# AdaLN block on one NeuronCore: latent scores in two row halves, first norm on ScalarE, new instruction lists and PSUM banks, expert weights mixed by quarters of the hidden layer

## The reference

```python
mod = (silu(c) @ wmod).reshape(32, 6, 1, 128)      # sa, ca, ga, sb, cb, gb
h = layernorm(x) * (1 + ca) + sa
x = x + ga * attn(h)
h = layernorm(x) * (1 + cb) + sb
x = x + gb * ffn(h)
# attn: 16 heads of 8, causal window of 32 over blocks of 32 keys, softmax;
#   8 latent heads: GQ = h@wgq, GK and GV = h@wgk and h@wgv pooled by 4 rows to 64 latents,
#   causal softmax over the latents, @ r_out_w; both gated by a sigmoid of Q, summed, @ w_out
# ffn: g = mean over rows of (relu(h@gate_w1.T + b) @ gate_w2.T + b2)      # 8 experts
#   mW1 = W1 + sum_e g[e] * TW1[e]   (512 x 128, one for each image)
#   mW2 = W2 + sum_e g[e] * TW2[e]   (128 x 512, one for each image)
#   out = gelu(h @ mW1.T + mb1) @ mW2.T + mb2
```

## Time and profile before

| | |
|---|---|
| median of 3 runs | 707.37 us (706.54 to 707.58) |
| the profiled execution: its own time | 706.55 us |
| the profiled execution: first to last instruction | 704.7 us, TensorE's clock granted at 0.983 of full on the mean |
| busy: PE, DVE, ACT, POOL | 662.0, 542.8, 382.1, 217.1 us |

### The profile page before, as it was taken

The page is one execution under the profiler, slowest core; times in us unless marked ns, Lnnn a source line. Parts: engine busy times, 40 slices in busy tenths (PEclk is TensorE's granted clock), DMA queues, the critical chain, the costliest instruction groups (busy, mean ns, idle before and its releaser), DMA issues.

```text
span 704.7 us, 24615 instructions
## 1 busy us (share of the span) xinstructions
PE 662.0 (94%) x9075; PEld 503.2 (71%) x9075; DVE 542.8 (77%) x1242; ACT 382.1 (54%) x907; POOL 217.1 (31%) x351
## 2 busy tenths in 40 slices
PE   4698999999999999999999999999869999999998
PEld 2365676667766667776667666677559899998996
DVE  5777898999998999999999989998757255472552
ACT  2264666567766577765677665677522423324232
POOL 3344444344533345443345443454320000000000
PEclk9799999999999999999999999999979999999999
DMA  4656410110011110101100101100500110000001
GB/s 108 170 79 87 57 31 22 30 30 22 22 30 24 34 24 22 30 22 28 32 22 22 30 22 30 30 15 16 74 3 2 30 32 7 30 22 30 30 8 52
DMA packets 65797, 24.84 MB, mean 35 GB/s; under 512 B 38440, under 2 KB 64360, under 8 KB 65648
## 3 DMA queue, kind: packets, MB, share of 16 engines
q1 hardware_dynamic: 64320, 18.25, 10.7%
q0 software_dynamic: 1456, 6.31, 5.8%
HBM read 16.13 MB, written 8.40 MB: 35 GB/s over the span
## 4 chain that ended last, share of the span: by engine, by line
PE 78%; DVE 16%; issue 3%; ACT 1%; DMA 0%; POOL 0%; DVEq 0%; SPq 0%; POOLq 0%
PE SB L822 8%; PE WB L810 8%; PE SB L889 7%; DVE rden L639 7%; PE WB L975 7%; PE WB L921 5%; PE WB L940 5%; PE WB L797 4%; PE WB L925 4%; PE SB L797 4%; DVE mx L553 3%; DVE Pr L560 3%; PE SB L1036 3%; PE WB L849 3%; PE WB L837 3%
## 5 line engine op out<-in xcount | busy, mean ns | idle before, releaser
L390 ACT ACTIVATE Pr<-Pr 128x512 f32<-128x512 f32 x128 | 77.8, 638 | 130.8 <-DVE Pr L560 130.6
L498 ACT ACTIVATE Pr<-WB,mb1T 128x256 f32<-128x256 f32 x128 | 49.8, 477 | 75.7 <-PE WB L810 75.6
L560 DVE TENSOR_TENSOR Pr<-SB,mx 128x512 f32<-128x512 f32 x128 | 84.9, 684 | 3.6
L553 DVE TENSOR_REDUCE mx<-SB 128x8 f32<-128x512 f32 x128 | 84.6, 682 | 3.8 <-PE SB L874 3.8
L364 POOL TENSOR_TENSOR attT<-a_gated,rem_g 128x256 f32<-128x256 f32 x32 | 23.2, 724 | 172.7 <-DVE a_gated L654 172.7
L395 ACT COPY PT<-SB 128x512 f32<-128x512 f32 x128 | 75.1, 589 | 2.1 <-PE SB L889 2.1
L639 DVE RECIPROCAL rden<-WB 128x256 f32<-128x256 f32 x32 | 56.2, 1758 | 22.0 <-PE WB L925 22.0
L335 POOL TENSOR_TENSOR KM<-K_ch,bd_scale 128x1024 f32<-128x1024 f32 x32 | 60.6, 1894 | 37.9 <-ACT K_ch L407 37.9
L889 PE MATMUL SB<-ident,Pr 128*128 128x128 f32 x512 | 66.8, 273 | 1.1 <-ACT Pr L390 1.0
L975 PE MATMUL WB<-GKBD,GQT 128*128 128x512 f32 (+1 forms) x128 | 56.4, 524 | 7.0 <-DVE wait_carrier L740 4.9
L889 PEld LDWEIGHTS SB<-ident,Pr 128*128 128x128 f32 x512 | 58.8, 141 | 5.1 <-ACT Pr L390 1.4
(11 more groups left out here) (188 smaller groups left out, 1419.7 us busy)
## 6 DMA issues: line engine op xcount, KB each, us to landing
x_all<-in_L_attn_x SPq DMA_DIRECT2D x32, 128.0 KB, 2.1
v_rows<-V_rows SPq DMA_DIRECT2D x32, 128.0 KB, 1.8
VBD<-v_rows SPq DMA_DIRECT2D x128, 32.0 KB, 1.8
TW<-in_L_ffn_TW POOLq DMA_DIRECT2D x16, 256.0 KB, 10.0
GA<-ga_rows POOLq DMA_DIRECT2D x1, 2048.0 KB, 11.8
out_x<-attT SPq DMA_DIRECT2D x16, 128.0 KB, 1.8
out_x<-y_ga SPq DMA_DIRECT2D x16, 128.0 KB, 1.8
PT<-in_L_ffn_W SPq DMA_DIRECT2D x2, 256.0 KB
```

The source lines that it names most:

```text
L390: nc.scalar.activation(Pr[:, k, :], Pr[:, k, :], ACT.Exp).then_inc(p_ready, 1)
L553: nc.vector.tensor_reduce(mx[:, k, :], SB[k][:].rearrange("p (h j) -> p h j", h=8), AX.X, ALU.max).then_inc(mx_ready, 1)
L560: nc.vector.tensor_tensor(Pr[:, k, :].rearrange("p (w h c) -> p h w c", w=2, h=8), SB[k][:].rearrange("p (h w c) -> p h w c", w=2, h=8), b ...
```

## The change

It rewrites most of the kernel, in these parts.

1. **First norm on ScalarE.** `xn_a` was two DVE `tensor_scalar`; it becomes two ACT activations, and POOL computes a shift for it (`inverse_std`, two more small operations).
2. **Latent projections and scores in two row halves.** `GQT` has the queries of rows 0 to 127 on partitions 0 to 63 and those of rows 128 to 255 on partitions 64 to 127. The mask becomes two bfloat16 products 32 rows deep, the scores two float32 products 64 rows deep.
3. **New lists and banks.** One list for each engine in another order, with a semaphore for each operation; the hidden gate layer uses WB1 in place of SB0. The sums of the softmax are still the products with `ones_bd`; the window's now carry a semaphore of their own (`den_done`).
4. **Expert weights by quarters.** Instead of 8 images x 512 hidden units the weights of 32 images x 128 hidden units are mixed at a time, in products 64 rows deep and 256 columns wide, alternately on the upper and the lower 64 rows. The output of a quarter is added to an accumulator in SBUF (`acc`, on memory that the attention no longer needs): ACT writes it in the first quarter, DVE adds in the other three. The first mix comes after the attention pipeline has ended. The stores are of two images each.
5. **Loads of the expert weights** go from POOL's queue (16 of them, six experts before the loop) to SP's (32, in steps 3 to 10).

```diff
 # tensor block, attention
-                mm(WB[1 - t][:, 0:8 * m].rearrange("p (h j) -> p h j", h=8), GQT[:, t * P:(t + 1) * P],
-                   GKBD[:, :, 0:m], start=True, stop=True).then_inc(ls_ready, 1)
+                    mm(to0, lat_sel[0:W, :], bc(lat_mask[0:W, 0:W], [W, LH, W], 1), start=True, stop=False, skip_group_check=True)
+                    mm(to1, lat_sel[W:NL, :], bc(lat_mask[W:NL, :], [W, LH, NL], 1), start=True, stop=False, skip_group_check=True)
+                    mm(to0, GQT[0:NL, :], GKBD[0:NL, :, 0:W], start=False, stop=True, skip_group_check=True).then_inc(ls0_done, 1)
+                    mm(to1, GQT[NL:P, :], GKBD[NL:P], start=False, stop=True, skip_group_check=True).then_inc(ls1_done, 1)
...
-                    bank_free(pe, it, (1, s_sub, 4, 1))
-                    mm(SB[0][:, 0:S], gate_w1T[:], h2T[:, bass.ds(b * S, S)], start=True, stop=True
-                       ).then_inc(hid_done, 1)
+                    bank_free(pe, it, (0, hT_ready, 1, 1), (1, ls0_sub, 1, 1), (2, plB_copied, 1, 1), (5, hid_summed, 1, 1))
+                    mm(WB[1][:, 0:S], gate_w1T[:], h2T[:, bass.ds(b * S, S)], start=True, stop=True).then_inc(hid_done, 1)
...
 # first norm: from DVE to ACT
-                    nc.vector.tensor_scalar(xn[:, t, :], src[:, t * D:(t + 1) * D], mv[:, t, 0:1], rstd[:, t:t + 1],
-                                            ALU.subtract, ALU.mult).then_inc(xn_s, 1)
+                        last = nc.scalar.activation(xn_a[:, t, :], x_all[:, bass.ds(b * S + t * D, D)], ACT.Identity,
+                                                    scale=rstd_a[:, t:t + 1], bias=shift_a[:, t:t + 1])
...
 # feed-forward, tensor block: new mix, ffn2 and order
+            def mix(c, part, kk):
...
+                for k in range(2 * kk, 2 * kk + 2):
+                    for r in range(2):
+                        rows = slice(HALF * r, HALF * r + HALF)
+                        lhsT = TW2[rows, k, c * P:(c + 1) * P] if part else TW1[rows, c * J + k, :]
+                        last = mm(SB[(2 * kk + r) % 4][:, (k % 2) * S:(k % 2 + 1) * S], lhsT,
+                                  Gd[rows].rearrange("p b j -> p (b j)"), start=True, stop=True)
...
+                    last = mm(WB[2 + n % 2][:, k * S:(k + 1) * S], mW2[:, b, :], u[b % 16], start=True, stop=True)
...
+            for c in range(FC):
+                for p in range(8):
+                    ffn1(c, p)
+                    if p % 2 == 0:
+                        mix(c, 1, p // 2)
+                for p in range(8):
+                    for q in (2 * p, 2 * p + 1) if p < 4 else (p + 4,):
+                        ffn2(c, q)
+                        if c == FC - 1 and q >= 2:
+                            final_T(q - 2)
+                    ffn1(c, 8 + p)
+                for kk in range(4):
+                    ffn2(c, 12 + kk)
+                    if c + 1 < FC:
+                        mix(c + 1, 0, kk)
...
 # feed-forward, DVE: the accumulator
+                    nc.vector.scalar_tensor_tensor(acc[b], WB[2 + n % 2][:, k * S:(k + 1) * S], gbT[:, b:b + 1], acc[b],
+                                                   ALU.mult, ALU.add).then_inc(acc_added, 1)
```

More of the change, by code:

```diff
@@ L178, in adaln_block @@
-        stored = [sem(f"stored{k}") for k in range(2)]
+                             "acc_begun", "acc_added", "fin_done", "o_ready", "stored"))
         def bc(ap, shape, *axes):
@@ L286, in _ @@
             step(2)
-            with sp.Fori(3, B - 1) as it:
+            for it in range(3, 3 + E):
+                step(it)
+                load_experts(it - 3)
+            with sp.Fori(3 + E, B - 1) as it:
                 step(it)
@@ L454, in step @@
-                if has(it, 1):
-                    latent_exp(it - 1, 0, PlA)
+                        last = nc.scalar.activation(xn_d[:, t, :], x_all[:, bass.ds(b * S + t * D, D)], ACT.Identity,
+                                                    scale=rstd_d[:, t:t + 1], bias=shift_d[:, t:t + 1])
+                    last.then_inc(xn_d_s, 1)
+                if has(it, 1):
+                    b = it - 1
+                    act.wait_ge(ls0_sub, b + 1)
+                    nc.scalar.activation(PlA[:], PlA[:], ACT.Exp).then_inc(plA_ready, 1)
@@ L776, in _ @@
+            for p in range(NPAIR - 2, NPAIR):
+                out_rows(p)
         @block.tensor
@@ new lines, in ffn1, with ffn2 @@
+            def ffn1(c, p):
+                n = c * NPAIR + p
+                if p == 0:
+                    pe.wait_ge(mixed, 16 * c + 8)
+                if n >= 2:
+                    pe.wait_ge(gelu_done, 2 * (n - 1))
+                for k in range(2):
+                    b = 2 * p + k
+                    last = mm(WB[n % 2][:, k * S:(k + 1) * S], mW1[:, b, :], h2T[:, b * S:(b + 1) * S], start=True, stop=True)
+                last.then_inc(ffn1_done, 1)
+            def ffn2(c, p):
+                n = c * NPAIR + p
+                if p == 0:
+                    pe.wait_ge(mixed, 16 * c + 16)
+                if 2 <= n < NPAIR + 2:
+                    pe.wait_ge(acc_begun, 2 * (n - 1))
+                elif n >= NPAIR + 2:
+                    pe.wait_ge(acc_added, 2 * (n - 1) - B)
+                pe.wait_ge(gelu_done, 2 * (n + 1))
+                for k in range(2):
+                    b = 2 * p + k
+                    last = mm(WB[2 + n % 2][:, k * S:(k + 1) * S], mW2[:, b, :], u[b % 16], start=True, stop=True)
+                last.then_inc(ffn2_done, 1)
@@ new lines, in final_T @@
+            def final_T(p):
+                pe.wait_ge(acc_added, B * (FC - 2) + 2 * (p + 1))
+                pe.wait_ge(mixed, 16 * FC)
+                if p >= 4:
+                    pe.wait_ge(o_ready, p - 3)
+                for k in range(2):
+                    for t in range(T):
+                        last = nc.tensor.transpose(SB[p % 4][:, (2 * k + t) * P:(2 * k + t + 1) * P],
+                                                   acc[2 * p + k][:, t * P:(t + 1) * P], ident[:])
+                last.then_inc(fin_done, 1)
@@ L1025, in step @@
                     last.then_inc(rem_done, 1)
-                if has(it, 1):
-                    gates(it)
-                if isinstance(it, int) and it == B + 3:
-                    for m in range(2, 4):
-                        mix(0, m)
                 if has(it, 4):
```

947 lines of the change are left out of this document (453 added, 494 removed).

## The result

The changed kernel takes **670.4 us** (median of 4 runs, 668.42 to 671.59), the kernel before in the same session 707.18 (706.54 to 707.58): a ratio of 0.9475, 95% interval [0.9454, 0.9497]. The forecast was 670 with a range of 642 to 694. The profiled execution of the changed kernel has a span of 669.9 us and a time of its own of 671.59.

A forecast was written before the change was run, and what follows sets the result against it. It took TensorE and DVE waiting in turn to bound the loop, and matmuls the feed-forward. 704.7 - 23.6 (loop) - 13.6 (hand-over and feed-forward) = 667.5 us span, hence 670 us measured; range 642 to 694.

The forecast's parts named there:

- `hid` on WB1: -0.82: Loop: `hid` ahead of the gates needs only `h2T`, so TensorE's waits of 0.18 and 0.64 us a step go.
- GQ projection in halves -0.21: Loop: two 256-column instructions become four of 128 writing separate column halves side by side, 0.21 us less a step.
- Latent scores -0.21: Loop: latent scores and masks go from 1.30 to 1.08 us by working side by side, 0.21 less a step.
- First norm to ACT: nothing is counted: Loop: DVE falls to about 13.0 us, ACT rises to 10.8, both under the step, so no gain.
- Switches +0.48 in the loop: Loop: tile shape changes 12 times a step instead of 8, at 0.12 us each, adding 0.48 us.
- A mix 1.10: Feed-forward: with row halves side by side, a mix of 8 instructions costs 0.86 us plus two switches, 1.10.
- PE waits at the ends of quarters 1 + 2 + 2: Feed-forward: TensorE waits for DVE 1 us at the first quarter's end and 2 in two others, +5.0.
- Hand-over: `hid`, ReLU and four small operations about 2.0: Between loop and feed-forward: last `hid`, its ReLU and four small dependent PE and DVE operations take about 2.0 us.
- The row halves on top of each other: Rival, mixes and latent scores: row halves do not work side by side; 711 us, slower than before; chance 0.07.
- Half-way there: Rival: two row halves give only 1.5, mixes cost 9 us and scores 4 more; 683 us; no chance given.
- `KM`: Rival, loop: the keys' mask on POOL becomes the loop's chain; step 14.8 us, total 688; chance 0.10.
- Better than counted: Rival: switches hidden and fewer register instructions between the semaphores; total 648 us; chance 0.11.

The follow-up runs named there:

- run 1: Changed kernel with both latent products and both halves of every mix forced onto rows 0 to 63: 726.61 us, ratio 1.0282 to the kernel before.
- run 2: Changed kernel with `hid` back on bank SB0 behind the gates, its ReLU behind the first exponential: 700.0 us, ratio 0.9900 to the kernel before.
- run 6: Changed kernel with the last image's norm statistics ahead of the first 28 images' expert step on DVE: 666.94 us, ratio 0.9419 to the kernel before.
- run 3: Kernel before with only `hid` moved to WB1 ahead of the gates, its ReLU ahead of the first exponential, in the loop: 697.18 us, ratio 0.9849.
- run 4: Changed kernel with the first norm's two scalings back on DVE, behind `PlB`'s subtraction: 697.51 us, ratio 0.9869 to the kernel before.
- run 9: Changed kernel with mixes ahead of `ffn2` at a quarter's end and DVE's additions ahead of its accumulations: 665.77 us, ratio 0.9396 to the kernel before.
- run 8: The kernel of run 7 with 14 unused products added where TensorE would wait: 660.69 us, ratio 0.9330 to the kernel before.
- run 5: Changed kernel with the first norm's two scalings on DVE, ahead of the latent reciprocal: 741.8 us, ratio 1.0496 to the kernel before.
- run 12: Changed kernel with the edits of run 7, run 8 and run 9, second-layer mixes in twos and an early one-element GELU: 651.83 us, ratio 0.9208.
- run 7: Changed kernel with one expert step for all 32 images, its bias products behind the first four mixes: 664.02 us, ratio 0.9364 to the kernel before.

## Why the prediction came out right, and where it did not

The side-by-side work of the row halves and the freed `hid`, on which the forecast rested, are both there, and each is needed (runs 1 and 2). That the sum is within 2.4 us of the span (667.5 against 669.9) is luck: its terms missed by up to 9 us, in both directions. Laid out from one landmark to the next:

- *To the last `hid`*: forecast 525.0 (527.0 less the 2.0 behind it) - 23.6 = 501.4, measured 492.55, 8.9 us earlier. The 27 steps between the first and the last of the loop, each 0.29 shorter than forecast, are 7.8 of it. The other 1.1 is the net of what stands ahead of the loop and behind it, and in that the late last norm (run 6) is a loss of some 4.4 us.
- *From there to the first mix*: forecast 2.0, measured 5.03, 3.0 late.
- *From there to the first `ffn1`*: forecast 6.1, measured 7.5, 1.4 late.
- *From there to the end*: forecast 158.0, measured 164.8, 6.8 late.

Step by step:

- *"`hid` on WB1: -0.82".* The mechanism is right and the releaser is gone. The stretch from `rem` over `hid` and the gates to the next product goes from 2.69 us (304.20 to 306.89) to 1.85 (312.15 to 314.00), 0.84 less. But that is the place where the wait stood, and not the price of the move: runs 2 and 3 put that at 0.40 to 1.04, depending on what is around it. Such a price is not a constant: a wait that goes is worth its length only if nothing waits just behind it, and in the old lists something did (run 3).
- *"GQ projection in halves -0.21".* Mis-sized. In the new step the four instructions take 0.27 us (301.03 to 301.30), which is about the side-by-side time. But the small product with `wgk` ran beside them before (307.95, the same start) and now stands behind them, so that the stretch went from 0.57 to 0.49 us: 0.08 less and not 0.21.
- *"Latent scores -0.21".* The stretch is 1.38 with its changes of shape, before it was 0.54 + 0.86 = 1.40 (296.81 to 297.35 and 298.69 to 299.55 in the trace of the kernel before). The forecast, with two changes at 0.12, was 1.32. Right within 0.06; with the changes of shape that it brings, the new form saves next to nothing by itself. It is still needed: the same products on the same rows cost 0.52 us more a step (run 1).
- *"First norm to ACT: nothing is counted".* The zero did the sum no harm, since in the sum TensorE never waits in the new step; the reason given for it failed. With everything else changed, the scaling at the better of two places on DVE costs 0.87 us a step, 27 us in all (run 4), of which some 0.35 a step may be POOL's doing. I had argued from DVE's busy share (13.0 us of 14.23), which leaves slack on average; but DVE's list is a chain with the reciprocal `rden` in it, and its idle time lies in other places than where the scaling is wanted. This 0.87 and the 1.04 of `hid` are together more than the 1.05 that the step gained: neither is a share of it, each is what goes wrong when that part alone is missing.
- *"Switches +0.48 in the loop".* By the landmarks the step lost 1.05 where 0.76 was forecast. Of the rest of TensorE's step, the transposes of `Pr`, the norms' transposes and the output product are 0.29 longer together. I put that down to the added changes of shape, which here stand beside 128-column instructions: some 0.3, less than counted. The latent value products (1.01 to 0.82), the queries' product and others are 0.4 shorter together, which no term of the sum had, and that is what made the step shorter than forecast.
- *"A mix 1.10" in the feed-forward.* The mix itself is 1.06, but the `ffn` behind it is 0.2 longer as well, so that a mix costs (39.7 - 27.65 - 1.38 - 0.32) / 8 = 1.29 (39.7 is a quarter, 27.65 its `ffn` instructions, 1.38 and 0.32 its waits). The step that failed is the price of a change of shape, 0.12 from 128-column rows: with 256-column instructions it is 0.20 (1.06 - 0.86, in both directions, and again in runs 1 and 9). 28 mixes x 0.19 = 5.3 us, most of the 6.8. The Trainium skill, page "TensorEngine Tiling (Array Packing)", section Key Properties, which the prediction weighed, says that a change of mode drains TensorE; the rows agree that a change costs time, and the estimate of 0.17 that I had set aside was the better one for the feed-forward.
- *"DVE addition 0.68".* Measured 0.69 (1.29 for two): right.
- *"PE waits at the ends of quarters 1 + 2 + 2".* It is 1.38 in all three, whether ACT or DVE accumulates. DVE's rate does not decide it: in the first quarter DVE itself waits 0.84 us ahead of each pair of additions, and in the others its two accumulations (0.92 from start to start) and two additions (1.21) come to 2.13 us, as much as TensorE takes for a mix and an `ffn2` (2 x 1.06). What is left is the delay from the last mix through two additions. Beside it stand 0.32 us ahead of each quarter's first `ffn2`. The sum, 3 x 1.38 + 4 x 0.32 = 5.4, comes near the 5.0 for another reason, by luck.
- *"Hand-over: `hid`, ReLU and four small operations about 2.0".* This failed in two ways. The clock: in the kernel before it falls to 0.50 here as well, but is back at 1.00 a few us later, with the first group's mixes to do. The kernel before:

```profile
515.00:520.00 5.00, 1.48 (x6) 0.83 (x5) 2.45 (x16) 0.88 (x2) 1.87 (x5) 0.50 0.00 0
525.00:530.00 5.00, 5.00 (x46) 4.95 (x45) 4.66 (x5) 1.13 (x3) 0.00 (x0) 1.00 0.01 3
```

Now it is at 0.50 through the whole expert step and until about 500.5 us, over more than half of the first three mixes. I had looked at the rows for their order and not for their clock. Run 8 prices it at 3.3 us. And the order on DVE: the last norm behind the first expert step, which I did not lay out, costs 4.4 us (run 6). It lies ahead of the last `hid`, so it is hidden in the first landmark.
- *The rivals.* The row halves on top of each other: excluded; the price by run 1 is 43.6 us, near the 41 that I gave, and 56 with the clock. Half-way there: excluded as well, as a mix less its change of shape (1.06 - 0.20) is the 0.86 of full overlap. `KM`: it ends at 309.79 and the mask products behind which the scores stand start at 310.36, no wait. DVE's additions at 1.06: excluded, 0.69. Better than counted: it came true in the loop, by 0.29 us a step, and not in the feed-forward.
- *The loads on SP's queue.* Counted at nothing. TensorE is busy 399.97 of the 400 us from 60 us on, so no loop step there lost anything to them.
- *"What the profile would show".* Four marks are as written: `hid` behind `rem`, the latent products (1.06 us to the next product, of which some 0.2 is the change of shape), the single mixes and `mixed_rows`. Three are not: the step is 13.94 and not 14.0 to 14.5, the run of mixes at half clock takes 4.75 us for three and not 3.6 for four, and TensorE's wait at a quarter's end is 1.38 and not some 2.

## What to carry to other kernels

Lay the new order out engine by engine at the seams of the program too, not only in the loop: ask what keeps TensorE busy while a chain of small operations runs, and what stands ahead of the last input on each queue. Don't price a moved operation by the busy share of the engine it leaves: ask at which place of the list it stands and whether that place is idle. And when two engines wait for each other in turn, a wait and the work around it have no prices of their own; undo each in turn, in the old kernel and in the new.

## What the hardware showed that was not expected

- A DVE scaling of float32 rows from SBUF to SBUF is held up by a POOL operation that runs at the same time. In run 5 two take 2.58 us instead of 0.60; the first takes 1.90 and ends at 303.94, behind POOL's `KM` (301.96 to 303.86). In run 4 the first takes 0.69 and ends at 310.07, behind POOL's `x_all` (309.26 to 309.99). POOL's operations keep their lengths (1.90 and 0.73); DVE's subtraction from PSUM into `PlB` shows no such thing: 0.68 us in run 4, where it starts at 308.78 under `KM` (307.41 to 309.31), and 0.67 in run 5 without it. The Trainium skill, page "SBUF — State Buffer", section "SBUF: two separate sides", says that GpSimd and a VectorE operation in a two-port mode, or one with two SBUF inputs, share a port pair, and that whichever starts first holds it for the whole instruction. The trace agrees as to who waits and for how long; in which mode the scaling ran no row shows.
- A change of tile shape costs about 0.1 us beside 128-column instructions (0.09 and 0.14 in the earlier trace rows) and 0.20 between 256-column ones, each way (1.06 - 0.86).
- 14 products whose result nobody reads make the kernel 3.3 us faster (run 8), 3.6 in run 12: the granted clock stays at 1.00 from 476 to 498 us, with short gaps, where run 7 has 0.77, 0.50 and 0.83 in three windows. In run 1 the clock is at 0.50 for 16 us in which TensorE has no gap; why is not shown.
